# Queries, keys and convolved projections of batches two to four, made ahead in the first scan with taps folded into the weights

## What is computed

```python
# first block: a state space mixer over ctx, gated by x
x  = einsum('bld,ed->bel', ctx, in_proj_w)                  # 512 channels
xc = conv_general_dilated(x, conv_w, padding=[(3, 0)], feature_group_count=512)   # 4 taps, causal
x  = silu(xc + conv_b[None, :, None])                       # called u in the kernel
...                                                         # low-rank projection, step sizes dt, scan over time
y  = y * silu(z)                                            # z: layer norm of the residual stream
# second block
query = einsum('bnc,dc->bnd', ctx, Wq) + bq
key   = einsum('bnc,dc->bnd', ctx, Wk) + bk
attention = softmax(einsum('bnd,bmd->bnm', query, key))     # applied to normalised rows
```

## Time and profile before

| | us |
|---|---|
| median of three runs (lowest, highest) | 956.47 (954.84, 959.32) |
| the profiled execution: its own time | 957.99 |
| its span in the trace | 956.2 |
| opening, to the first scan (start of DVE's L1304) | 31.2 |
| first scan, to DVE's last sum (L1446) | 123.6 |
| first turning and between, to the second scan | 84.4 |
| the same between the second and the third scan, and the third and the fourth | 87.8 and 83.3 |

### The profile page before, as it was taken

How to read it: one execution, slowest core, us unless ns; L and a number is a source line. 1 busy time by engine, 2 the same in 40 slices (tenths; PEclk the granted TensorE clock), 3 DMA queues, 4 the chain that set the end, 5 groups by cost and what they waited for, 6 DMA issues and landing times. The chain is left out here.

```text
span 956.2 us, 9268 instructions
## 1 busy us (share of the span) xinstructions
PE 817.1 (85%) x2789; PEld 405.3 (42%) x2789; DVE 778.0 (81%) x905; ACT 647.5 (68%) x975; POOL 520.8 (54%) x425
## 2 busy tenths in 40 slices
PE   6621347999899998999899998998999997898999
PEld 2110023454344444444334444444444444447887
DVE  3899889886899998975989998978899998853333
ACT  5899879774688863773689863775689864623442
POOL 0798794203999881213999891116998861022000
PEclk9755558899999998999999999999999999999999
DMA  8279982001499981301599981301799960201221
GB/s 304 39 146 235 278 160 44 1 1 46 94 222 222 241 190 44 111 0 45 110 219 227 232 192 33 111 1 45 159 219 230 205 177 22 89 1 45 98 101 66
DMA packets 46817, 119.55 MB, mean 125 GB/s; under 512 B 5792, under 2 KB 6944, under 8 KB 46256
## 3 DMA queue, kind: packets, MB, share of 16 engines
q0 software_dynamic: 16128, 58.73, 32.8%
q1 hardware_dynamic: 30640, 60.24, 18.3%
HBM read 56.03 MB, written 4.19 MB: 63 GB/s over the span
## 5 line engine op out<-in xcount | busy, mean ns | idle before, releaser
L1702 POOL TENSOR_TENSOR work<-du,bcast 128x1024 f32<-128x1024 f32 x128 | 358.1, 2872 | 28.2 <-DVE du L1338 28.1
L1304 DVE TENSOR_TENSOR_SCAN pair<-pair,work 128x512 f32<-128x512 f32 x256 | 299.1, 1214 | 20.4 <-ACT pair L899 16.8
L899 ACT ACTIVATE pair<-dt,a_neg 128x512 f32<-128x512 f32 x256 | 165.9, 681 | 30.9 <-DVE work L1311 28.0
L665 PE MATMUL bank<-stage,ring 128*128 128x512 f32 x384 | 176.4, 603 | 2.9 <-ACT stage L1135 2.4
L1311 DVE TENSOR_TENSOR work<-pair,ccast 128x1024 f32<-128x1024 f32 x128 | 156.8, 1225 | 11.5
L1717 POOL DMA_DIRECT2D u<-work x112 | 132.1, 1179 | 39.3 <-DMA u<-work 23.1
L443 PE MATMUL bank<-xd,pick 128*128 128x512 bf16 x128 | 55.2, 431 | 69.4 <-ACT bcast L884 41.8
L665 PEld LDWEIGHTS bank<-stage,ring 128*128 128x128 f32 x384 | 73.5, 193 | 86.8 <-issue 77.3
L1688 POOL TENSOR_SCALAR fst<-fst 128x1 f32<-128x1 f32 x32 | 8.9, 278 | 167.5 <-DVE fst L1538 167.2
L681 PE MATMUL bank<-ring,stage 128*128 128x512 f32 x192 | 88.1, 608 | 0.0
L545 PE MATMUL pair<-w1q,qT 128*128 128x512 bf16 x256 | 62.1, 393 | 5.6 <-ACT qT L1113 5.6
(11 more groups left out here) (172 smaller groups left out, 1473.7 us busy)
## 6 DMA issues: line engine op xcount, KB each, us to landing
u<-work POOLq DMA_DIRECT2D x112, 512.0 KB, 6.0
ring<-ffn_dram SPq DMA_DIRECT2D x120, 256.0 KB, 4.7
ring<-ffn_dram SPq DMA_DIRECT2D x16, 512.0 KB, 3.2
xres<-x_dram SPq DMA_DIRECT2D x4, 1024.0 KB, 6.0
stage<-w_dram SPq DMA_DIRECT2D x1, 4096.0 KB, 16.5
stage<-w_dram SPq DMA_DIRECT2D x4, 1024.0 KB, 7.6
out_dram<-stage SPq DMA_DIRECT2D x16, 256.0 KB, 2.1
ctxT<-ctxT_dram SPq DMA_DIRECT2D x4, 512.0 KB, 7.8
```

The source lines that it names most:

```text
L665: last = pe.matmul(banks[UP_BANKS[f % 3]][:], piece(b, f)[:, k * P:(k + 1) * P], xnT[:, k, :], start=k == 0, stop=k == J - 1)
L899: act.activation(pairs[s % DECAYBUFS][:, q, :], dt[:, p * HALF + q, :], ACT.Exp, scale=a_neg[:, p * HALF + q, n:n + 1]).then_inc(s_decay, 1)
L1304: dve.tensor_tensor_scan(pair[:, q, :], pair[:, q, :], rows[:, q, :], 0.0, ALU.mult, ALU.add).then_inc(s_scan, 1)
L1702: pool.tensor_tensor(work[:, s % SCANBUFS, :, :], du[:, p * HALF:(p + 1) * HALF, :], bcast[:, n % 2, :].unsqueeze(1).broadcast_to([P, HALF ...
```

## The change

Three things are done.

**Folded taps.** At the opening POOL writes for each 128 channels a diagonal per tap (`tap_diagonals`, in `hT`), PE multiplies them by ones (`tap_rows`), and DVE multiplies the input projection by these rows (`fold`, into `ring`). A convolved projection is then 8 matmuls (4 taps, 2 halves of the contraction) accumulated in one bank, each tap shifted by a column, and needs no `convolve`.

**Units made ahead.** For each of the batches two to four there are six units: four of these, and query and key of two matmuls each. They are 108 matmuls in 18 units. `spread()` lays them over the places of the first scan from (4, 1) to (11, 3), four and three at a time by turns. ACT copies each with its bias to `hT` at the next place (`unit_copy`), SP stores it to device memory (`prepared`). Their contexts lie in `hx`. `load_prepared` brings queries and keys to `xpad` and the convolved projection to `u` for the pass that needs them; `project`, `project_copy`, `convolve`, `qk_products` and `qk_copy` stay for batch 0 alone.

**What moved to make room.** The layer norm sums of batch 0 go from ACT in slot 6 to DVE in slot 5 (`gate_stats`), the scaling of `b2` from the opening to slot 6. `weight_mean` uses bank 0 and holds PE until ACT has read it. The eight first pieces of `ring` wait for the last unit. All 56 filler matmuls stand in `first_turning`, behind a wait for the last copy.

```diff
+def unit_size(e):
+    return TAPS * KC if e % UNITS < J else KC
+def spread():
+    places = [(4, 1), (4, 2), (4, 3)] + [(slot, i) for slot in range(5, SLOTS) for i in range(4)]
+    parts, evictions, e, done = {}, {}, 0, 0
+    for n, place in enumerate(places):
+        room = 4 - n % 2
...
 # SP
-            load_context(1)
+                elif k == 0:
+                    sp.wait_ge(s_unit, (B - 1) * UNITS)
...
+            def store_unit(e):
+                sp.wait_ge(s_evict, e + 1)
+                sp.dma_start(prepared[e // UNITS, e % UNITS], hT[:, e % 4, :]).then_inc(s_spill[e % 4], 16)
...
+            def load_prepared(m):
+                sp.wait_ge(s_y, m * 2)
...
+                sp.dma_start(qk, prepared[m - 1, J:].rearrange("i p l -> p i l")).then_inc(s_qkin, 16)
+                sp.wait_ge(s_yT, m * T)
+                sp.dma_start(u[:], prepared[m - 1, 0:J].rearrange("j p l -> p j l")).then_inc(s_uin, 16)
...
 # PE
+            def tap_rows(j):
+                pe.wait_ge(s_diag, j + 1)
+                pe.matmul(banks[ROW_BANKS[j]][:], ones[:], hT[:, j, :], start=True, stop=True).then_inc(s_rows, 1)
+            def unit(e, first, last):
...
+                    else:
+                        pe.wait_ge(s_evict, e - 1)
+                for n in range(first, last):
+                    if i < J:
+                        shift, k = divmod(n, KC)
+                        ins = pe.matmul(bank[:, shift:], folded(i, k)[:, TAPS - 1 - shift, :], ctx_in[:, k, 0:L - shift],
+                                        start=n == 0, stop=n == TAPS * KC - 1)
...
             def first_turning(m):
-                keep_awake(24)
-                keep_awake(16)
+                pe.wait_ge(s_evict, (B - 1) * UNITS)
+                keep_awake(56)
...
             def weight_mean(i, n):
                 pe.wait_ge(s_wsq, 4 * i + 4)
+                pe.wait_ge(s_bcc, bc_index(n + 2, 0) + 1)
...
+                pe.wait_ge(s_wms, i + 1)
 # ACT
             def silu_u(b):
-                act.wait_ge(s_conv, b * J + J)
+                act.wait_ge(s_uin, b * 16)
...
 # DVE
             def opening(m):
                 for j in range(J):
-                    convolve(m, j)
-                gate_bias()
+                    convolve(j)
+                fold(0)
+                fold(1)
                 split(m)
                 step_inputs(m, 0)
+                fold(2)
                 step_inputs(m, 1)
+                fold(3)
             def between(b, m):
                 h_scale(b, 0)
                 h_scale(b, 1)
                 h_quant(b, 0)
-                convolve(m, 0)
-                convolve(m, 1)
                 h_quant(b, 1)
-                convolve(m, 2)
-                convolve(m, 3)
                 second(b, 0)
...
 # POOL
+            def tap_diagonals(j):
+                pool.tensor_tensor(hT[:, j, :].rearrange("p (t d) -> p t d", t=TAPS),
+                                   ident[:].unsqueeze(1).broadcast_to([P, TAPS, P]),
+                                   pch[:, j, 0:TAPS].unsqueeze(2).broadcast_to([P, TAPS, P]), ALU.mult).then_inc(s_diag, 1)
+            pool.wait_ge(s_first, first_wait)
+            for j in range(J):
+                tap_diagonals(j)
```

More of the change, by code:

```diff
@@ L62 @@
 ATT_BANKS = (4, 6, 7, 6)
-MEAN_BANK = 2
+MEAN_BANK = 0
+ROW_BANKS = (4, 7, 2, 3)
+UNITS = 6
 GATE_BANKS = (1, 0, 4, 5)
@@ L90, in bc_index @@
     return min(2 * n + 2, 2 * NS - 1) if i else max(2 * n - 1, 0)
+def unit_size(e):
[5 more added lines that the diff above has]
+        room = 4 - n % 2
+        while room and e < (B - 1) * UNITS:
+            take = min(room, unit_size(e) - done)
+            parts.setdefault(place, []).append((e, done, done + take))
+            done, room = done + take, room - take
+            if done == unit_size(e):
+                evictions.setdefault(places[n + 1], []).append(e)
+                e, done = e + 1, 0
+    return parts, evictions
+UNIT_PARTS, UNIT_COPIES = spread()
 def in_parts(ap):
@@ L234, in program @@
         s_ctx = sem("s_ctx")
+        s_ctxin = [sem(f"s_ctxin{m}") for m in range(1, B)]
+        s_diag = sem("s_diag")
+        s_rows = sem("s_rows")
+        s_fold = sem("s_fold")
+        s_unit = sem("s_unit")
+        s_evict = sem("s_evict")
+        s_spill = [sem(f"s_spill{c}") for c in range(4)]
+        s_uin = sem("s_uin")
+        s_qkin = sem("s_qkin")
         s_x = sem("s_x")
@@ L471, in project, with units @@
                 last.then_inc(s_inproj, 1)
+            def tap_rows(j):
+                pe.wait_ge(s_diag, j + 1)
+                pe.matmul(banks[ROW_BANKS[j]][:], ones[:], hT[:, j, :], start=True, stop=True).then_inc(s_rows, 1)
+            def unit(e, first, last):
+                m, i = e // UNITS + 1, e % UNITS
+                bank, ctx_in = banks[2 + e % 2], ctx_of(m)
+                if first == 0:
+                    if i == 0:
+                        pe.wait_ge(s_ctxin[m - 1], 16)
+                    if e < 2:
+                        pe.wait_ge(s_fold, 3 + e)
+                    else:
[5 more added lines that the diff above has]
+                                        start=n == 0, stop=n == TAPS * KC - 1)
+                    else:
+                        ins = pe.matmul(bank[:], wqk[:, n, i - J, :], ctx_in[:, n, :], start=n == 0, stop=n == KC - 1)
+                if last == unit_size(e):
+                    ins.then_inc(s_unit, 1)
+            def units(slot, place):
+                for e, first, last in UNIT_PARTS.get((slot, place), ()):
+                    unit(e, first, last)
             def keep_awake(n, bank=3):
@@ L844, in pass_ @@
                         f_unit(b, slot, 2)
+                    else:
+                        units(slot, 2)
                     bcast_next(m, slot, 1, 1)
@@ L848, in pass_ @@
                         f_unit(b, slot, 3)
+                    else:
+                        units(slot, 3)
                 if rest:
@@ L1094, in quarter @@
             def quarter(b, slot, i, rest):
-                if slot == (ZSTAT_SLOT - 1 if rest else ZSTAT_FIRST):
+                if rest and slot == ZSTAT_SLOT - 1:
                     gate_sum(b, i)
-                if slot == (ZSTAT_SLOT if rest else ZSTAT_FIRST):
+                if rest and slot == ZSTAT_SLOT:
                     gate_mean(b, i)
@@ L1188, in pass_ @@
                     copy_next(m, slot, 0, 0)
+                    if not rest:
+                        unit_copies(slot, 0)
                     quarter(m, slot, 0, rest)
                     attention(m, prev, slot, 0, 0)
-                    if slot == QK_SLOT:
-                        qk_copy(m, prev, 0)
+                    if slot == QK_SLOT and not rest:
+                        qk_copy(0)
                     if rest:
@@ L1199, in pass_ @@
                     copy_next(m, slot, 0, 1)
+                    if not rest:
+                        unit_copies(slot, 1)
                     quarter(m, slot, 1, rest)
                     attention(m, prev, slot, 0, 1)
-                    if slot == QK_SLOT:
-                        qk_copy(m, prev, 1)
+                    if slot == QK_SLOT and not rest:
+                        qk_copy(1)
                     if rest:
@@ L1207, in pass_ @@
                     copy_next(m, slot, 1, 0)
+                    if not rest:
+                        unit_copies(slot, 2)
                     quarter(m, slot, 2, rest)
@@ L1213, in pass_ @@
                     copy_next(m, slot, 1, 1)
+                    if not rest:
+                        unit_copies(slot, 3)
                     quarter(m, slot, 3, rest)
```

173 lines of the change are left out of this document (106 added, 67 removed).

## The result

| | before | after |
|---|---|---|
| device time, median of 4 runs | 956.88 us (954.84 to 959.32) | 982.09 us (978.06 to 983.08) |
| profiled execution, span | 956.2 us | 980.7 us |
| opening, to the first scan | 31.19 | 34.54 |
| first scan, to the last sum | 123.60 | 144.65 |
| last sum to `first_sum` | 5.39 | 12.57 |

The change made the kernel slower by 2.5% (ratio 1.0254, 95% interval 1.0217 to 1.0292). The forecast was slower by 0.5%, with a range that ended at 970. The stretches are cut at the starts of DVE's rows; `second` is DVE's first sum with a result of `down1`. Of the 24.5 us between the two spans the opening has 3.4, the first scan 21.1, its end 7.2, the three betweens -9.6 and everything else 2.5. The first scan is where the forecast failed: 5.9 us had been expected there.

A forecast was written before the change was run, and what follows sets the result against it. DVE was taken to bound the opening and first scan, PE the betweens, DVE close behind. -12.8 + 0 + 5.0 + 6.1 - 0.2 + 6.3 = +4.4 on 957.99 gave 962.4, less 1.5 for the median: 960.9; range 949 to 970.

The forecast's parts named there:

- Stalls in the first scan, -0.2 us: First scan: PE keeps pace at 3.6 us against 3.56; 3.3 us of new stalls against 3.5 gone; bounds -4 and +6.
- The rows of ACT: First scan, slots 7 to 9: ACT has no room for its added copies, taken as 3.3 us of new stalls.
- POOL's two old stalls: Late first scan: two DVE stalls on POOL, 3.5 us, taken as gone, with loads leaving the stretch of DMA share 1.05.
- DVE in the first scan, +6.1 us: First scan: three counted layer norm sums 2.8 us, three tensor_scalar operations about 1, waits for POOL 2.3; bounds 3 and 10.
- Opening, +5.0 us: Opening: POOL's diagonals hold up the convolution by 3.8 us, and fold 3 before the first scan adds 1.2.
- End of the first pass, +6.3 us: End of first pass: all 56 fillers wait for the last copies and take 14.2 us, delaying DVE; bounds 4.5 and 7.5.
- Betweens, -12.8 us: Three betweens: the second transpose_h starts 4.26 us earlier each time, PE then waiting three microseconds for DVE; bounds 9 and 15.
- Queries and keys out of slot 4: Slot 4 of later passes: PE loses two pairs of 1.88 us, ACT two copies of 0.6; gain taken as 0.
- loads: Second and third between: load_prepared may bring `u` up to 6 us late for ACT's silu; taken as 0.
- the rival that had it going: Later scans: the early DVE stall goes without query and key products, 3 x 2.6 = 7.8 us, 953.1; chance 0.25, alone or with free port.
- The slower one (late `u`, or ACT full): Silu waits 3 us twice for `u`, or stalls in slots 7 to 9 are 6 us more: 967; chance 0.21.
- The one with PE bound in the scan, at 0.04: First scan: at the lower clock 108 matmuls take 190 us against 124 of the scan, about 1,020; chance 0.04.

The follow-up runs named there:

- the run with the lean units: The changed kernel with six of the eight matmuls of each folded unit left out, all copies, stores and waits kept: 971.85 us (1.0150).
- the experiment: The changed kernel with POOL's four products in the opening cut from 128x512 to 128x8: 979.09 us (1.0223).
- placed otherwise: The changed kernel with units dealt evenly, port waits and clock mended, 128 rows in step_sizes, end of first pass reordered: 948.37 us, ratio 0.9897 to the kernel before.

## Why the prediction was wrong, step by step

- **Stalls in the first scan, -0.2 us: the step that failed.** Measured +9.2 us of DVE not busy. The working compared averages: 3.6 us of PE for a place of 3.56, "So PE holds". An average with no slack says nothing about an engine that issues in order. Three kinds of place had no room. Slot 4 has two places without a half step, so eleven matmuls came in a row (3.70 us). Neighbouring short units wait for each other's bank (3.34). `weight_mean` waits for late squares, with units between it and the next row (2.27). The rows of ACT were read as the risk, 3.3 us; in the run with the lean units its copies made no stall over 0.95 us, though ACT was full beside them. That POOL's two old stalls would go, 3.5 us, was right in size. The reason given, the DMA share, isn't borne out: it is 1.06 from 110 to 120 us in the changed kernel too, and why they went stays open.
- **DVE in the first scan, +6.1 us: mis-sized.** Measured 11.9. The statistics came out at about 0.94 each as read, but the first, too, counted: the stall that should have hidden it remained (1.51 us). The waits for POOL were taken at 1.17 us each, half a product; they were 2.7 and 5.1. The nearest row for such a wait showed 2 us, and a short operation can wait until two products are done.
- **Opening, +5.0 us.** Measured +3.35: 2.7 for the convolution beside POOL's products instead of 3.8, of which the experiment returned all, and 1.2 for fold 3, less 0.4, by which the convolution began earlier, and a little at the second `du`. The mechanism held.
- **End of the first pass, +6.3 us.** Measured +7.2, with 13.95 us of fillers where 14.2 had been read from the earlier trace rows. The mechanism held.
- **Betweens, -12.8 us.** Measured -9.6. Up to the second `transpose_h` the betweens gain 4.9, 4.1 and 3.5 us, 12.5 in all, and the wait of PE was named; what it does to the clock was not. From there to `second` each takes 1.3 to 1.6 us more, 4.5 in all, and eight fillers gave back 1.1 to 1.7 each time. The falls of the clock at `step_sizes` add luck: the kernel before has one worth 3.3 us in its second between, the changed one only 1.7 in its first. Without them the gain would be 8.0.
- **Queries and keys out of slot 4, and loads, 0 each.** Scans 2 to 4 are 0.3 to 0.9 us longer, and the early stall of the second is 3.29 us, where it was 2.57; the rival that had it going fell. `u` was not late: ACT's silu of it followed its table load without a wait.
- **Rivals.** The slower one (late `u`, or ACT full) had the right sign and the wrong engine. The one with PE bound in the scan, at 0.04, was the nearest to what happened, but it priced a low clock over the whole scan; the clock was high (0.94) but for the places behind PE's waits, and PE set the pace all the same, by its queue. Its chance rested on the clock alone.

## What to carry to other kernels

When work is added to an in-order engine that another engine waits for, add up what stands between two results for which the other engine waits, at the worst place, and not the mean of all; look for places without their usual partner, and for waits (a bank, a sum) in front of the added block. An elementwise operation in SBUF can cost many times its own length beside a GpSimd that computes back to back (a `tensor_scalar` 5.57 us instead of 0.48), so it belongs where GpSimd rests; the layer norm statistics, 0.69 us beside POOL, showed no such wait. The placement decides: the same idea gave +2.5%, and placed otherwise -0.4% against a kernel before that has the 128 rows as well.

## What the runs showed of the hardware

The granted clock of PE fell from 1.00 to 0.50, its lower level of 1.2 GHz, in and behind eight float32 records of matmuls over 16 rows, in 14 of 33 betweens; in the one shown above PE was busy 4.00 of 4.00 us. With the same matmuls over 128 rows, zeros added, it stayed at 1.00 in 12 of 12, and four records took 1.94 us against 1.98. The Trainium skill ("TensorE: Matmul & The Clock Gate", section "Part 1: The HAM clock gate") has the clock follow from how busy PE has been; here the records of busy time did not tell the two cases apart, and the number of rows did. Why the fall hits one between and not the next stays open; it moved with edits tens of microseconds ahead.

A DVE operation with a single 128x4 input took 2.87 us beside one product of POOL, though its record begins 0.19 us ahead of that product's, and one of 128x512 took 5.57 us, until two products were done. In both cases POOL's issue of a DMA overlaps the start of the product that went ahead. A wait that outlasts the instruction that caused it had not been expected.
